# Cross attention and a mixture of experts: sorted rows scattered in every head step in place of two steps in three

## The reference, cut to what matters

```python
x = x + xattn(layernorm(x), ctx_1024, ctx_1024, mask, Wq, Wk, Wv, Wo, 16)
# ffn(layernorm(x)):
scores = sigmoid(xt @ gate_w.T)
_, idx = top_k(scores + gate_b, 4)
w = take_along_axis(scores, idx); w = 2.5 * w / sum(w)
y = sum_e comb[:, e] * (silu_and_mul(xt @ w13[e].T) @ w2[e].T)   # w scattered to comb
y = y + silu_and_mul(xt @ w13_s.T) @ w2_s.T
```

## Time and profile before

| | us |
|---|---|
| three runs | 2245.89, 2254.79, 2255.83 |
| their median | 2254.79 |
| the profiled execution's own time | 2257.12 |
| its span in the trace | 2255.2 |
| TensorE busy | 2096.2 |
| VectorE busy | 1879.3 |
| ScalarE busy | 1680.7 |
| GpSimd busy | 1410.9 |

### The profile page before, as it was taken

How to read it: one execution, slowest core, us unless ns; L and a number is a source line. 1 busy time by engine, 2 the same in 40 slices (tenths; PEclk the granted TensorE clock), 3 DMA queues, 4 the chain that set the end, 5 groups by cost and what they waited for, 6 DMA issues and landing times. The chain is left out here.

```text
span 2255.2 us, 58109 instructions
## 1 busy us (share of the span) xinstructions
PE 2096.2 (93%) x16576; PEld 2020.2 (90%) x16576; DVE 1879.3 (83%) x6129; ACT 1680.7 (75%) x4795; POOL 1410.9 (63%) x2107
## 2 busy tenths in 40 slices
PE   6999999999999999999999999998898998888885
PEld 5999999999999998999999999997788897888884
DVE  6999999999999999999999999998753446666677
ACT  5988889888888888889888888988554554444431
POOL 3565655555555555878888877885655545555556
PEclk9999999999999999999999999999999999999998
DMA  6777777777777767866666656666766667788797
GB/s 190 186 176 187 191 178 187 183 183 190 174 193 177 183 173 180 218 175 176 171 179 181 174 158 166 176 167 184 248 237 226 237 234 266 261 273 276 248 309 238
DMA packets 261295, 457.32 MB, mean 203 GB/s; under 512 B 36544, under 2 KB 148672, under 8 KB 260992
## 3 DMA queue, kind: packets, MB, share of 16 engines
q1 hardware_dynamic: 235376, 383.07, 61.0%
q0 software_dynamic: 25616, 70.55, 9.8%
HBM read 141.00 MB, written 144.70 MB: 127 GB/s over the span
## 5 line engine op out<-in xcount | busy, mean ns | idle before, releaser
L773 POOL TENSOR_SCALAR E<-E,rinv 128x256 f32<-128x256 f32 x1024 | 481.1, 481 | 458.3 <-DVE rinv L1084 454.0
L959 ACT ACTIVATE E<-E,negmax 128x256 f32<-128x256 f32 x1024 | 508.7, 502 | 4.9 <-DVE negmax L1109 4.7
L1109 DVE CUSTOM_DVE_ANT_0 E<-pS,m_in 128x256 f32<-128x256 f32 x1024 | 387.1, 415 | 35.6 <-PE pS L870 32.4
L1128 DVE TENSOR_TENSOR PT_lo<-pT,PT_hi 128x512 fp32r<-128x512 f32 x512 | 350.5, 684 | 27.5 <-ACT PT_hi L977 23.3
L1529 POOL DMA_INDIRECT block<-expert_rows,slot x256 | 245.3, 958 | 185.6 <-PE epG L87 95.2
L977 ACT ACTIVATE PT_hi<-pT 128x512 fp32r<-128x512 f32 x512 | 304.8, 595 | 9.3 <-PE pT L880 0.3
L880 PE MATMUL pT<-ident,E 128*128 128x128 f32 x2048 | 306.6, 272 | 0.5 <-POOL E L773 0.5
L893 PE MATMUL pV<-PT_hi,V 128*128 128x256 f32 x1024 | 287.4, 303 | 6.4 <-DVE PT_lo L1128 6.4
L869 PE MATMUL pS<-qk_st 128*128 128x256 f32 x1024 | 268.6, 284 | 8.6 <-DMA qk_st<-qk_sp 8.4
L945 ACT ACTIVATE qk_sp<-pj 128x256 fp32r<-128x256 f32 x512 | 196.8, 385 | 104.2 <-PE pj L87 89.1
L870 PE MATMUL pS<-qk_st,qk_sp 128*128 128x256 f32 x1024 | 266.2, 282 | 0.0
(11 more groups left out here) (218 smaller groups left out, 7139.3 us busy)
## 6 DMA issues: line engine op xcount, KB each, us to landing
qk_st<-qk_sp SPq DMA_DIRECT2D x512, 192.0 KB
qk_st<-qk_sp SPq DMA_DIRECT2D x512, 128.0 KB
sorted_rows<-qk_st SPq DMA_DIRECT2D x152, 256.0 KB, 3.6
xg<-sorted_rows SPq DMA_DIRECT2D x76, 512.0 KB
expert_rows<-block SPq DMA_DIRECT2D x76, 512.0 KB
acc<-x_plus_attention SPq DMA_DIRECT2D x35, 256.0 KB
x_in<-in_x SPq DMA_DIRECT2D x32, 256.0 KB
c_in<-in_ctxT SPq DMA_DIRECT2D x32, 256.0 KB, 4.1
```

Source lines behind the costliest of these rows:

```text
L773: last = pool.tensor_scalar(e[:, t, :], e[:, t, :], rinv[:, r, t:t + 1], 1.0, ALU.mult, ALU.mult)
L959: last = act.activation(E[r][:, t, :], E[r][:, t, :], ACT.Exp, bias=negmax[:, r, t:t + 1], scale=-1.0, accum_out=rowsum[:, r, t:t + 1])
L1109: last = dve.tensor_tensor_reduce(out=E[r][:, t, :], in0=pS[g % 2][:, t, :], in1=m_in.tile(b)[:, t, :], scale=-1.0, scalar=BIG, op0=ALU.ad ...
L1128: dve.tensor_tensor(lo[:, :, :], pT[n % 2][:, :, :], f32(hi[:, :, :]), ALU.subtract).then_inc(s_ptlo, 1)
```

## The change

One constant of the planner: the distance between two scatters in attention is one step and not one and a half.

```diff
@@ -385,7 +385,7 @@
     SET_FROM = [(SET_BATCHES * s + SET_BATCHES + 1) * H + LG_STEP + 1 for s in range(SETS - 1)]
     RANK_STEP = 10
     RANKS_AT = [(GROUP_START[g + 1] + 2) * H + RANK_STEP for g in range(EARLY_GROUPS)]
-    SCATTER_STEPS = 1.5
+    SCATTER_STEPS = 1.0
     scatter_at, step = {}, 0.0
     for b in range(GROUP_START[EARLY_GROUPS]):
         g = sum(b >= start for start in GROUP_START[1:GROUPS])
```

## The result

The changed kernel is slower: 2264.95 us (median of 7 runs, 2260.4 to 2272.07) against 2250.54 for the kernel before (7 runs, 2245.89 to 2255.83), a ratio of 1.0067, 95% interval 1.0049 to 1.0085. The forecast was 2250, in the range 2239 to 2268: the time is inside the range, but it moved the other way, by 14 us more in place of 7 less. The profiled execution took 2272.07 us, its span is 2269.8, 14.6 more than before.

A forecast was written before the change was run, and what follows sets the result against it. Attention was taken as bound by TensorE, with units beside indirect DMAs slowed by 0.34 us a scatter. Units gain 10.9 us, attention loses 4: -6.9 us against the profiled 2257.12 gives 2250 us, range 2239 to 2268.

The forecast's parts named there:

- Attention bound by TensorE, scatters free there: Attention: TensorE busy 566.36 of 570.09 us without scatters, 331.17 of 333.26 with; a scatter costs 0.01 us.
- GpSimd full at 16 a batch, loss 4 us: Attention: GpSimd needs 47.1 to 48.5 us a batch against TensorE's 47.5; loss 4 us, bounds 0 and 25.
- the transpositions of the probabilities: Attention, three steps behind scaling: TensorE would wait there for GpSimd about 3 us in total, where it was 0.5.
- SyncE's loads at nothing: SyncE's queue in attention: loads waiting for scatters to land delay head stacks at no cost; at worst 22 us.
- the first rival: Attention, scaling of the probabilities: GpSimd becomes the bound, 2.3 to 3 us a batch, 2271 to 2279 us; chance 0.17.
- The sum that gave a margin of 0.5 us: SyncE's queue in attention: the scatter's landing leaves SyncE free by 1126.5, 0.5 us before its next stack.
- The 32 scatters moved give 10.9 us: Expert units: 32 scatters moved into attention save 0.34 us each, 10.9 us; bounds 0 and 19.
- the remaining 80 keep their price: Expert units: scatters still there cost 0.34 us each, though group 2 is planned at three units a batch.
- The mean rate: Expert units: remaining scatters at 0.6 a us match the gathers' rate (182 in 298 us), where the price was the same.
- the forecast's own signs of being wrong: TensorE's wait for GpSimd passes 15 us, units beside scatters still take 210 us, or price not in proportion to count.
- Price per indirect DMA: Expert units: excess over 2.80 us a unit is 0.34 us per scatter, 0.36 per gather, taken as an indirect DMA's price.
- The rival that the excess is not the scatters': Expert units: stops come by themselves, so nothing is gained and 4 us lost in attention, 2261 us; chance 0.12.

The follow-up runs named there:

- f4: Changed kernel with a scatter every 1.25 steps in attention, 12.8 a batch in place of 16; ratio to the kernel before 0.9990, attention 680.4 us.
- the fitted kernels: Five versions of the changed kernel: scatters every 1.4 steps (group 0) and 1.25 (group 1), loads 4 steps ahead; attention 681.6 to 684.1 us.
- h3: Changed kernel with three short GpSimd memsets after each scatter beside the units; ratio to the kernel before 0.9936, units 6 to 67 in 173.3 us.
- k1: Changed kernel, scatters every 1.4 and 1.25 steps, loads 4 steps ahead, group 2 4.5 units apart, one memset after each scatter in the units; ratio 0.9994.
- f3: Changed kernel with loads 4 steps ahead instead of 8 and group 2's batches planned 4.5 units apart instead of 3; ratio to the kernel before 0.9976.
- e4: Kernel before with group 2's batches planned 3 units apart instead of 4.5; ratio to the unedited kernel before 1.0002.
- f1: Changed kernel run again unaltered beside the kernel before; ratio 1.0071, units 6 to 67 in 220.6 us.

## Why the prediction was wrong

- **Attention bound by TensorE, scatters free there** (rows 2 and 3): right at 10.7 scatters a batch, and in f4's trace at 12.8; the fitted kernels, at up to 12.8, lie 2.2 us higher.
- **GpSimd full at 16 a batch, loss 4 us**: GpSimd is full, and the size is near. Measured 6.9 us in the profiled executions and 6.2 in the means, of which some 4 go with the scatters and not with SyncE. But the path was not the one forecast: I put the loss at the transpositions of the probabilities, 3 us of waiting there, and it is 0.5; GpSimd's wait for the reciprocal fell by 29 us over the run (454.0 to 424.7), not 50. Where on TensorE the 4 us fall is not settled: the views show them in small waits of different names. So that 4 stands for 4 may be luck.
- **SyncE's loads at nothing**: mis-sized. The term was 0, with up to 22 us inside the first rival; later loads took some 2.3 us off attention's time; TensorE's waits for stacks are 8.3 us where they were 0.9. The sum that gave a margin of 0.5 us held only for a scatter that is not late itself.
- **The change of stage** had no term; it cost 2.0 us. With the last scatter at 1560.1 for 1530.4 us GpSimd comes later to its first work of the units. In all traces it goes with the number scattered in attention: 22.6 to 23.3 us with 176, 21.0 to 22.1 with 160, 20.4 to 21.7 with 144; that GpSimd's lateness is the reason is argued from the times and not tested.
- **The 32 scatters moved give 10.9 us**: this is the step that failed, in its sentence that the remaining 80 keep their price though their plan is "faster than GpSimd issues them". I had worked out 13 us a batch against three units a batch and drawn from it only that nobody waits for the end. But the pace of the units was what kept the scatters apart. Without it the price went to 0.69 us a scatter in the dense part, and the units lost 7.6 us. The mean rate, by which I argued for the same price, is the wrong measure: what counts is how closely the scatters follow each other (h3, k1) and, as the trace before suggests below, how many do so in a row. With an even plan the step's number nearly holds (f3: 202.3 us, and I had said 201). Two of the forecast's own signs of being wrong came true: the units beside scatters took over 210 us, and the price was not in proportion to the count.
- **The trace before had it.** Gate activations of the kernel before, around three units and at the start of a fourth:

```profile
1654.20 0.39 ACT L1672 ACTIVATE gate_act<-epG 128x256 f32<-128x256 f32 x1 [0.78 <-PE epG L87]
1663.60 0.38 ACT L1672 ACTIVATE gate_act<-epG 128x256 f32<-128x256 f32 x1 [1.47 <-PE epG L87]
1687.84 0.39 ACT L1672 ACTIVATE gate_act<-epG 128x256 f32<-128x256 f32 x1 [0.78 <-PE epG L87]
```

The three units from 1654.20 to 1663.60, each beside one pair of scatters, take 9.40 us, 1.0 more than 3 x 2.80: 0.17 us a scatter. The one unit from 1687.84 to 1696.27, beside a row of seven, takes 8.43 us, 5.6 more: 0.80 a scatter. My 0.34 was the mean of cheap pairs and dear rows, and the plan decides how many of each there are. (This is read from one trace; no run varied the length of the rows alone.)

- **Price per indirect DMA**, 0.34 and 0.36: the equality of the two rows did not show a constant of an indirect DMA, since a scatter's price is 0 in two series, and with pauses too. The rival that the excess is not the scatters' is out (h3), but its doubt about an unseen cause was the right one to price.
- **Chances**: slower had 0.17, for the rival that GpSimd binds attention. The slower outcome came by a way that no rival named, a dense plan in the units.

## What to carry to other kernels

Moving work out of a stage also moves the plan of what stays: see whether the pacing that kept the rest apart still bites. A queue that is planned faster than it can issue is not harmless because nobody waits for its end; look at how closely its instructions follow each other, and at who stops meanwhile. A price that is the mean over a stretch should be split by what happens there, here pairs and rows, before it is carried over to another plan. And a load on a shared queue whose release comes one step before it, not five, should be priced with the releasing engine late.

## What was not expected of the hardware

- Where the excess is present, TensorE's results reach ScalarE late beside a row of indirect DMAs of GpSimd at a pitch of 1.27 us, in the stop shown not before 1.1 us after the last of them (11.6 us for the unit beside ten scatters, 24 us for two units beside 18 gathers). At a pitch of 1.46 us the stretch loses as much; at 2.0 to 2.2 us nothing. In attention, where the pitch is 2.2 us at the least and 2.9 in the median, TensorE is busy for 671.78 of 686.59 us, which leaves no room for stops like these.
- The same program took 2152 us in two series and 2250 to 2262 in the others, with the whole difference in the expert stage. In those two series the dense plan, with 98 scatters in the stretch, cost nothing (e4, 173.2 us). The runs don't say what differs.
- The scatters themselves lasted no longer where others stood still: 77.08 us for 80 in f1, 94.43 for 98 in e4, 63.99 for 66 in h3, 0.96 to 0.97 us each with the excess and without. The Trainium skill (SBUF — State Buffer, section "SBUF: two separate sides") describes a lock on the port pair that VectorE and GpSimd share: while VectorE runs an operation in a 2-port mode, GpSimd cannot write its DMAs' descriptors. That would hold up GpSimd's own DMAs. The traces give no sign of it, since the scatters' durations are the same with the excess and without; what came late was TensorE's results.
